# Flamingo block with gated attention and experts on one core: stacks of Q and K in another layout, and VectorE's normalisation of x at other head slots

## What is computed

```python
x = x + tanh(g_xattn[0]) * xattn(layernorm(x), ctx_1024, Wq, Wk, Wv, Wo, bo)
x = x + tanh(g_ffn[0]) * ffn(layernorm(x), ...)

def xattn(x, context, Wq, Wk, Wv, Wo, bo):        # 16 heads of 32
    q = x @ Wq.T; k = context @ Wk.T; v = context @ Wv.T
    scores = einsum('bhqd,bhkd->bhqk', q, k) / sqrt(32)      # causal
    probs = softmax(scores)
    y = einsum('bhqk,bhkd->bhqd', probs, v)
    return y @ Wo.T + bo
```

## Time and profile before

| | |
|---|---|
| median of 3 runs | 1925.9 us (1924.12 to 1927.26) |
| the profiled execution | 1926.66 us, its span 1924.9 us |
| busy share: PE, PE's weight loads, DVE, ACT, POOL | 97%, 82%, 79%, 50%, 36% |
| DMA packets, bytes | 151,494, 182.8 MB, of which under 2 KB 115,872 |
| mean granted clock of TensorE | 0.994 of full speed |

### The profile page before, as it was taken

One profiled execution on the slowest core, in us unless ns is written; L12 is line 12 of the kernel. 1 busy time (PEld: TensorE's weight loads), 2 busy tenths in 40 slices (PEclk: granted clock), 3 DMA queues, 4 the chain that ended last, 5 costly groups with the idle time before them and its releaser, 6 DMA issues.

```text
span 1924.9 us, 33464 instructions
## 1 busy us (share of the span) xinstructions
PE 1872.5 (97%) x11664; PEld 1588.0 (82%) x11664; DVE 1513.8 (79%) x3345; ACT 970.2 (50%) x2284; POOL 698.4 (36%) x939
## 2 busy tenths in 40 slices
PE   6999999999999899999999999999999999999999
PEld 6899998889999678888878888877888887888887
DVE  5888888888888887777788777787777778877776
ACT  4777777777777744243343333353334334423332
POOL 3132233232233533334433344353334453333330
PEclk9999999999999899999999999999999999999999
DMA  7565556656566231221123212114122112312111
GB/s 213 124 148 132 148 147 144 156 128 160 149 146 162 67 121 44 77 77 46 54 75 112 74 58 67 55 33 147 51 77 67 55 56 66 112 53 65 45 44 44
DMA packets 151494, 182.81 MB, mean 95 GB/s; under 512 B 11424, under 2 KB 115872, under 8 KB 151328
## 3 DMA queue, kind: packets, MB, share of 16 engines
q1 hardware_dynamic: 151328, 180.68, 33.4%
HBM read 111.43 MB, written 18.87 MB: 68 GB/s over the span
## 4 chain that ended last, share of the span: by engine, by line
PE 75%; DVE 13%; issue 5%; ACT 3%; POOL 3%; SPq 1%; DMA 1%; DVEq 0%; POOLq 0%; ACTq 0%
PE gate_up L1234 31%; PE down L1748 18%; PE bank L741 14%; PE probs_t L872 3%; PE scores L842 2%; DVE ops_lo L1091 2%; DVE acc L1599 2%; PE bank L731 1%; POOL hidden L1447 1%; DVE probs L673 1%; PE y L861 1%; PE y L859 1%; PE down L1727 1%; SPq L353 1%; DVE pt_lo L705 1%
## 5 line engine op out<-in xcount | busy, mean ns | idle before, releaser
L1234 PE MATMUL gate_up<-xo_hi,ops_hi 128*128 128x512 f32 x1120 | 440.0, 393 | 13.2 <-DVE hidden L1210 4.4
L1234 PE MATMUL gate_up<-xo_lo,ops_hi 128*128 128x512 f32 x1120 | 436.1, 389 | 0.0
L1234 PE MATMUL gate_up<-xo_hi,ops_lo 128*128 128x512 f32 x1120 | 436.1, 389 | 0.0
L1234 PEld LDWEIGHTS gate_up<-xo_hi,ops_hi 128*128 128x128 f32 x1120 | 210.2, 188 | 67.2 <-DVE gated L1210 9.6
L1599 DVE SCALAR_TENSOR_TENSOR acc<-down,scale,acc 128x512 f32<-128x512 f32 x320 | 238.1, 745 | 34.8 <-PE down L1748 34.4
L1748 PE MATMUL down<-d_hi,h_hi 128*128 128x512 f32 x640 | 249.1, 389 | 0.0
L1748 PE MATMUL down<-d_hi,h_lo 128*128 128x512 f32 x640 | 249.0, 389 | 0.0
L1748 PE MATMUL down<-d_lo,h_hi 128*128 128x512 f32 x640 | 249.0, 389 | 0.0
L1234 PEld LDWEIGHTS gate_up<-xo_lo,ops_hi 128*128 128x128 f32 x1120 | 210.2, 188 | 44.3
L1234 PEld LDWEIGHTS gate_up<-xo_hi,ops_lo 128*128 128x128 f32 x1120 | 210.3, 188 | 42.3
L1447 POOL TENSOR_TENSOR hidden<-hidden,gated 128x512 f32<-128x512 f32 x120 | 157.4, 1319 | 189.8 <-DVE hidden L1215 170.4
(11 more groups left out here) (179 smaller groups left out, 4586.2 us busy)
## 6 DMA issues: line engine op xcount, KB each, us to landing
g_raw<-in_w_gate SPq DMA_DIRECT2D x40, 512.0 KB, 3.9
u_raw<-in_w_up SPq DMA_DIRECT2D x40, 512.0 KB, 3.9
d_raw<-in_w_down SPq DMA_DIRECT2D x40, 512.0 KB, 3.7
k_stack<-k_hi SPq DMA_DIRECT2D x128, 128.0 KB, 2.6
q_stack<-q_hi SPq DMA_DIRECT2D x128, 128.0 KB, 2.6
c_in<-in_ctx_t SPq DMA_DIRECT2D x16, 512.0 KB, 3.8
x_in<-in_x SPq DMA_DIRECT2D x16, 512.0 KB, 3.8
k_stack<-k_lo SPq DMA_DIRECT2D x64, 128.0 KB, 2.6
```

The costliest lines, as they stand in the source:

```text
L1234: ins = pe.matmul(gu_ps[bank][:], ops[x][:, which, a, c, :], xo[y][:, b, c, :], start=(begins and c == 0 and i == 0), stop=(c == CH - 1 an ...
```

## The change

Four edits, all in `attention`. The stacks get the shape [P, JH, C, S] in place of [P, H, S], so that one transfer writes 4 KB to each of 32 partitions in one run and not in four runs of 1 KB; a head's columns are found at `s % JH, s // JH`. `LN_SLOT` goes from 5 to 7 and `XN_SLOT` from 13 to 10: DVE's statistics and its normalisation of x, and POOL's refinement of 1/std with the former (in POOL's list the bias of slot 6 now comes before it). And PE waits for v_rest of the sequence before, ahead of K's first projection in iterations 0 and 1.

```diff
     def stacks(i):
-        return sb(f"q_stack{i}", [P, H, S], F32R), sb(f"k_stack{i}", [P, H, S], F32R)
+        return sb(f"q_stack{i}", [P, JH, C, S], F32R), sb(f"k_stack{i}", [P, JH, C, S], F32R)
...
-    LN_SLOT, C_SLOT, XN_SLOT = 5, 12, 13
+    LN_SLOT, C_SLOT, XN_SLOT = 7, 12, 10
...
-                return sp.dma_start(dst[lo:hi, j:H:JH, :].bitcast(F32), src[j * DH:(j + 1) * DH].bitcast(F32))
+                return sp.dma_start(dst[lo:hi, j].bitcast(F32), src[j * DH:(j + 1) * DH].bitcast(F32))
...
                             wait(pe, x1_made, n.times(T, 1 - 3 * T))
+                            if n.k in (1, 2):
+                                pe.wait_ge(v_rest_made, T * n.k)
...
-                            ins = pe.matmul(sc_ps[s % 2][:, t, :], q_stack[par][pairs, s, tile(t)],
-                                            k_stack[par][pairs, s, :], start=True, stop=True)
+                            ins = pe.matmul(sc_ps[s % 2][:, t, :], q_stack[par][pairs, s % JH, s // JH, tile(t)],
+                                            k_stack[par][pairs, s % JH, s // JH, :], start=True, stop=True)
```

## The result

The changed kernel takes 1934.3 us in the median of 5 runs (1931.9 to 1935.2); before took 1925.9. The ratio is 1.0041, with a 95% interval of 1.0030 to 1.0052: slower by 0.41%, some 8 us, where +5.1 us (1931.0) was forecast. A second series of the same program gave 1.0043 (1.0029 to 1.0057). The profiled execution took 1934.19 us.

The account below looks back on a forecast made before the run. PE (TensorE), busy 97% of the span, was taken as the bound. Slots +9.5, tail -4.5, opening +0.8 and layout -0.7 sum to +5.1 us; against the median of 1925.9 that gave 1931.0 us, range 1925.0 to 1937.0.

Parts of the forecast that it names:

- the tail: End of iteration 0, paced by DVE and ScalarE: normalisation at slot 10 leaves the path, -4.5 us (-2.5 to -5.5).
- the opening: Iteration -1: q_lo's second half 1.3 us later delays c_lo and K's projection, +0.8 us (0 to +1.5).
- Statistics in front of q_lo: Slot 7, iterations 1 to 13: moved statistics delay q_lo and PE's transposes of y; slots together +9.5 us (6.7 to 10.5).
- iteration of the first kind: Iterations 1, 2, 3, 12 and 13, which normalise no rows of x1: 1.18 us lost in each.
- they fit into slot 7: Faster rival: statistics fit slot 7, the eight old q_lo waits go, none comes; -13.0 us, 1912.9 us, chance 0.13.
- Iteration 0 has no y to transpose and pays nothing: Statistics at slot 7 of iteration 0: no transposes of y wait behind q_lo, so cost 0.
- The clock behind the tail: After iteration 0's tail, 76 to 82 us: keeping the upper clock level, 2.0 us taken, bounds 0 and 3.0.
- no wait over 1 us for neg_max: Sign at 73 us, in iteration 0's tail: no such wait, and a clock of 1.00 behind it.
- The normalisation in steady iterations: Two instructions at slot 10, expected 2 x 0.535 = 1.07 us, fit without costing PE anything.
- a collision in slot 10: Slower rival: normalisation delays t_lo of slot 11, PE waits 0.8 us in 13 iterations; 1941 us, partly 1936, chance 0.15.
- The wait for v_rest, put at nothing: PE's added wait in iterations 0 and 1: its operation ends before the opening's late c_lo, so 0.
- The layout: Stacks in 4 KB runs: 0 in steady work; iteration 14's last x_t may land sooner, -0.7 us, up to 2.1.

Follow-up runs that it names:

- e_ln7: The statistics moved to slot 7 alone, on the kernel before (old stacks, normalisation at slot 13): 1938.2 us, ratio 1.0062.
- e_xn10: The normalisation moved to slot 10 alone, with the wait for v_rest, on the kernel before: 1921.0 us, ratio 0.9972.
- e_first5: The changed kernel with its statistics at slot 5 in iterations -1 and 0 only: 1932.3 us, ratio 1.0026.
- n_split3: The changed kernel with one bn_stats at slot 5, the other at slot 6, the rest of the statistics at slot 7: 1913.2 us, ratio 0.9926.
- n_ln8xn11: The changed kernel with statistics at slot 8 and normalisation at slot 11: 1935.9 us, ratio 1.0054.
- e_split: The kernel before with its statistics cut: two bn_stats at slot 5, the six short ones at slot 7: 1919.8 us, ratio 0.9966.
- e_layout: The new stacks and the added wait for v_rest on the kernel before, statistics and normalisation unmoved: 1925.8 us, ratio 0.9999.
- n_ln5xn10: The changed kernel with its statistics back at slot 5, new stacks and normalisation at slot 10 kept: 1921.5 us, ratio 0.9976.

## Why the prediction was right, and where it was off

The direction was right and the time lies in the range, 3 us above the value. In the spans it is +7.6 against +5.1: the tail gave 1.9 us less than forecast and the end cost 1.9 that had no term, while the opening, iteration 14, the slots and the experts' part took back 0.2 to 0.6 each. So the nearness of the sum owes something to terms that cancel. By its own steps:

- **Statistics in front of q_lo: right.** +9.5 was forecast for the slots, 9.25 and 9.41 were measured; 1.24 against 1.18 in each iteration of the first kind, 0.37 against 0.45 in the others (between the bounds of 0.1 and 0.5). e_ln7 shows that the statistics alone do it. The rival "they fit into slot 7" had one thing right, as the runs with the cut statistics show: VectorE has idle time enough there, but for half the block.
- **"Iteration 0 has no y to transpose and pays nothing": wrong.** The moved statistics cost 0.2 us there by themselves (e_ln7), but beside the normalisation at slot 10 they cost 2.2 to 2.5, through VectorE's arrears. The tail's term was -4.5; the normalisation alone gives -4.8 (e_xn10), and with the moved statistics it gives 2.3 to 2.6. I had taken the two edits for independent in the one place where VectorE is the pace. e_first5 shows it: slot 5 in the first iterations alone restores 4.8. This is 2 us of the miss.
- **The clock behind the tail: the bound was right, the value was not reached.** 2.0 us were taken for it; without the moved statistics it is 2.5, with them about 1. The sign named beforehand, no wait over 1 us for neg_max, came true (0.89 us at 73.18), and yet the clock behind it did not stay at 1.00.
- **The normalisation in steady iterations: right.** L597 has a median of 541 ns in the changed kernel as in e_xn10, and e_xn10 lags by 0.01 us over iterations 1 to 13, so the rival of a collision in slot 10 is out.
- **The opening: right in its chain, and within its scatter.** The second half of q_lo starts 0.98 us later than before (32.34; 1.3 was taken), and K's projection starts behind a wait for c_lo, at 40.33 where 40.5 was forecast:

```profile
37.75 2.52 POOL L445 TENSOR_TENSOR c_lo<-c_in,c_hi 128x1024 fp32r<-128x1024 f32 x1 [0.42 <-ACT c_hi L479]
```

```profile
38.06 0.50 PE L844 MATMUL scores<-k_stack,q_stack 96*128 96x256 f32 x2 [1.96 <-DMA q_stack<-q_hi]
...
40.33 0.38 PE L741 MATMUL bank<-c_hi,w_hi 128*128 128x256 f32 x1 [1.76 <-POOL c_lo L445]
```

  It cost 0.24 us in one trace and 2.31 in the other; +0.8 was forecast, with 0 to 1.5 as its ends, too narrow for the second. Of the 2.07 between the two traces, 1.09 are there already at the first half of q_lo (26.90 and 27.99), ahead of the moved statistics on VectorE. The wait for v_rest, put at nothing, shows in no list of TensorE's waits.
- **The layout: wrong reason, size within its bounds.** -0.7 was tied to x_t's landing. The changed kernel does gain 1.04 us in iteration 14, and its wait there fell from 2.09 to 0.2 us:

```profile
DVE v_rest L681 <- POOL v_parts L453: 0.2, 1, 0.2
```

  But the new stacks alone keep the wait at 2.3, and every kernel with old stacks and another order gains there as well (0.60 to 0.77 us). Most of the gain goes with the order of the slots, not with the stacks. How the order brings it about was not tried, and not every order gains: n_split3 loses 0.34 us there with a wait of 2.4.
- **The end of the attention: no term, 1.9 to 2.0 us.** It went with the clock in most kernels: all with a mean of 0.88 in 620:690 lose 1.6 to 2.0 us between iteration 15 and the last x_res, and those with 0.98 (e_xn10, n_ln8xn11, e_split) gain 0.9. But of the two with 0.90, e_layout gains 0.1 and n_ln5xn10 loses 2.7, so the mean clock is not all of it, and no run shows that it is the cause. Which order gives which clock stays open. The order of e_xn10 gave 0.98 with the old stacks and 0.90 with the new ones, though the series of both have the same ratio; over the seven runs of e_xn10 the mean clock of the whole run lay between 0.993 and 0.997 and the time between 1918.8 and 1922.8.

In the medians the parts add up better than in the traces: 0.62% for the statistics, -0.28 for the normalisation, -0.01 for the stacks make 0.33, and 0.41 to 0.43 were measured. The rest, about 0.1% or 1.5 to 1.9 us, is near the interaction in the tail (2.2 to 2.5 us, less the 0.2 that the statistics cost alone), as far as intervals of 0.1% each allow.

## What to carry to other kernels

Where one engine follows another closely, ask of a moved block not how long it takes in all but what stands directly behind it and which engine waits for that in the same slot; a block that doesn't fit costs its excess, and the same work cut into pieces of a slot's idle time can cost nothing (2.33 us in one piece: +9.3 us at slot 7; cut in three over slots 5 to 7: -8.8). Two edits that are each free or worth something alone meet where the engine they load is the pace, so sum them there in time order, not as separate terms. And look for the edit that gains inside a change that loses: here the normalisation alone is worth 0.28%.

## What the runs showed of the hardware

VectorE's instructions of L597, 512 columns each, took 1.35 us in the median at slot 13, where from iteration 0 on GpSimd's c_lo and third part of V run beside each for 1.1 to 1.4 us, and 0.54 at slot 10, where GpSimd runs beside each for 0.3 us at most. So the place of an instruction changed its length by a factor of 2.5. This was foreseen from the least of the old durations. Not foreseen was how much hangs on TensorE's clock in a kernel that is busy for 97%: in e_xn10 half of the tail's gain (2.5 of 4.8 us) came where the clock was 1.00 in place of 0.50, and one and the same program spread over 4 us with mean clocks of 0.993 to 0.997. An edit worth 2 us can be read here from a stage in which the clock stays at its upper level (iterations 1 to 13, steady to 0.2 us) and hardly from the whole time.
